# A mixer's opening: c's first convolution on other engines, first products in other banks, x's first turns behind the next x product

## What is computed

```python
proj = input_states @ in_proj_w.T              # 512 -> gate | x | B | C | dt
gate, xBC, dt = proj[..., :INTER], proj[..., INTER:INTER + CONV], proj[..., INTER + CONV:]
xBC = silu(causal_conv(xBC, conv_w, K=4) + conv_b)     # each channel by itself, 4 taps
hs, Bm, Cm = split(xBC)                        # x: 128 heads x 64;  B, C: 8 groups x 128
dt = softplus(dt + dt_bias);  cum = cumsum(dt * A)
scores = (C_i . B_j) * exp(cum_i - cum_j) * dt_j       # causal, for each head
y = scores @ x + D * x
g = rms_norm_by_group(y * silu(gate)) * norm_w
out = g @ out_w.T
```

## Time and profile before

| | us |
|---|---|
| median of 3 runs | 1915.48 (1914.93 to 1915.66) |
| profiled execution, its own time | 1914.4 |
| its span | 1912.7 |
| TensorE busy in the span | 1817.4 |
| GpSimd busy | 1434.0 |
| vector engine busy | 1340.3 |
| ScalarE busy | 1163.2 |

### The profile page before, as it was taken

The page is one execution under the profiler, slowest core; times in us unless marked ns, Lnnn a source line. Parts: engine busy times, 40 slices in busy tenths (PEclk is TensorE's granted clock), DMA queues, the critical chain, the costliest instruction groups (busy, mean ns, idle before and its releaser), DMA issues.

```text
span 1912.7 us, 29241 instructions
## 1 busy us (share of the span) xinstructions
PE 1817.4 (95%) x10780; PEld 1454.2 (76%) x10780; DVE 1340.3 (70%) x1703; ACT 1163.2 (61%) x2105; POOL 1434.0 (75%) x1429
## 2 busy tenths in 40 slices
PE   6998897878999999999999999999999999999977
PEld 4776675667887888888888888888888888888866
DVE  5664564666767777687668767876777687678656
ACT  3222432358676777676676757766777577676752
POOL 4312333638997999799969978997899799979972
PEclk9997997989999999999999999999999999999999
DMA  3000001013222222222222222222322223213201
GB/s 111 1 2 23 2 1 59 12 55 104 90 83 83 78 94 100 67 90 88 89 78 78 94 72 86 94 91 70 96 78 94 72 89 99 95 62 115 72 23 44
DMA packets 107025, 135.54 MB, mean 71 GB/s; under 512 B 9026, under 2 KB 74690, under 8 KB 106884
## 3 DMA queue, kind: packets, MB, share of 16 engines
q1 hardware_dynamic: 105924, 133.63, 21.3%
q10 hardware_dynamic: 960, 0.05, 0.0%
HBM read 131.02 MB, written 2.62 MB: 70 GB/s over the span
## 4 chain that ended last, share of the span: by engine, by line
PE 78%; DVE 2%; POOL 1%; issue 1%; ACT 1%; DVEq 0%; POOLq 0%; ACTq 0%
PE ps L144 20%; PE ps L146 20%; PE ps L145 20%; PE ps L1928 7%; PE ps L1885 3%; PE ps L1929 3%; PE ps L1074 2%; PE ps L1913 1%; PE ps L1946 1%; PE ps L1948 0%; DVE mix_xT L1667 0%; DVE mix_u L1791 0%; PE ps L116 0%; POOL ffn_ln_mv L72 0%; DVE mix_xnT_lo L132 0%
## 5 line engine op out<-in xcount | busy, mean ns | idle before, releaser
L144 PE MATMUL ps<-mix_xnT_hi,mix_w_hi 128*128 128x512 f32 x1152 | 463.1, 402 | 9.5 <-DVE mix_bT L1667 9.5
L146 PE MATMUL ps<-mix_xnT_hi,mix_w_lo 128*128 128x512 f32 x1152 | 455.5, 395 | 0.0
L145 PE MATMUL ps<-mix_xnT_lo,mix_w_hi 128*128 128x512 f32 x1152 | 455.1, 395 | 0.0
L1667 DVE SCALAR_TENSOR_TENSOR mix_xT<-ps,mix_cur,mix_xT 128x510 f32<-128x510 f32 x378 | 279.2, 745 | 144.1 <-ACT mix_xT L1482 135.1
L1393 POOL TENSOR_SCALAR_AFFINE_SELECT mix_spread<-mix_spread 128x256 f32<-128x256 f32 x512 | 305.7, 631 | 0.0
L1687 DVE TENSOR_TENSOR mix_decay<-mix_decay,mix_cb 128x1536 f32<-128x1536 f32 x128 | 293.8, 2333 | 4.9 <-ACT mix_decay L1508 4.7
L1531 ACT ACTIVATE mix_g_hi<-mix_gated 128x512 fp32r<-128x512 f32 x128 | 81.0, 633 | 328.3 <-POOL mix_gated L1370 173.2
L144 PEld LDWEIGHTS ps<-mix_xnT_hi,mix_w_hi 128*128 128x128 f32 x1152 | 217.8, 189 | 58.4 <-issue 11.1
L146 PEld LDWEIGHTS ps<-mix_xnT_hi,mix_w_lo 128*128 128x128 f32 x1152 | 217.4, 189 | 50.9
L145 PEld LDWEIGHTS ps<-mix_xnT_lo,mix_w_hi 128*128 128x128 f32 x1152 | 217.9, 189 | 47.1
L1506 ACT ACTIVATE mix_decay<-mix_spread,mix_cur_ncum 128x256 f32<-128x256 f32 x512 | 253.7, 495 | 0.0
(11 more groups left out here) (262 smaller groups left out, 3327.0 us busy)
## 6 DMA issues: line engine op xcount, KB each, us to landing
mix_spread<-cum_rows SPq DMA_DIRECT2D x128, 512.0 KB, 4.0
mix_w_raw<-in_w_in_stream SPq DMA_DIRECT2D x144, 256.0 KB, 4.2
mix_wo_raw<-in_w_out_T SPq DMA_DIRECT2D x64, 256.0 KB, 3.6
att_w_raw<-in_w_attn_T SPq DMA_DIRECT2D x12, 256.0 KB, 4.1
x<-in_x SPq DMA_DIRECT2D x8, 256.0 KB, 4.4
out_rows<-x SPq DMA_DIRECT2D x8, 256.0 KB, 2.1
att_wp_raw<-in_w_proj_T SPq DMA_DIRECT2D x4, 256.0 KB, 2.6
mix_bT<-in_w_ffn_T SPq DMA_DIRECT2D x2, 512.0 KB, 4.9
```

Of the source, the lines that this page charges most:

```text
L144: pe.matmul(out, lh, rh, start=(k == 0), stop=False)
L145: pe.matmul(out, lh, rl, start=False, stop=False)
L146: last = pe.matmul(out, ll, rh, start=False, stop=(k == tiles - 1))
L1667: dve.scalar_tensor_tensor(out=d[:, :, shift:T], in0=src[:, :, 0:T - shift], scalar=w[:, MK - 1 - shift:MK - shift], in1=d[:, :, shift:T], ...
```

## The change

Six things change, all in the opening (group 0, up to pair 0's x and B·C):

1. dt's turns go into banks 0, 1, 0, 1 instead of 6, 7, 4, 5; each waits for what that bank held (B's taps, or the copy of the turn before it).
2. Products 3 and 4 are issued by a new function `lead_product`, into banks 6, 7 and 4, 5, ahead of dt's turns.
3. C's taps 1 to 3 leave the vector engine: ScalarE scales each tap from the bank into one of four spare SBUF halves (`scale_c`), GpSimd adds it to `cT` (`add_c`). The semaphores are renumbered, so that `convolved` and `tapped` no longer count C.
4. x's turns (`turn_x`) move from ahead of the body to behind product 5.
5. In pair 0 of group 0 ScalarE takes x1's first tap ahead of the exponentials; the vector engine scales x (`scale_x`) and copies B·C 0 and 1 between x1's two halves of taps.
6. GpSimd's order: splits 3 and 4, two additions, split 5, four additions, split 6, then the body.

```diff
-        DT_BANKS = (6, 7, 4, 5)
+        DT_BANKS = (0, 1, 0, 1)
+        c_tapped, c_scaled, c_added = sem("c_tapped"), sem("c_scaled"), sem("c_added")
+        C_TAPS = [(half, shift) for half in range(2) for shift in range(1, MK)]
+        tapped_c = [ap[:, n * 512:(n + 1) * 512] for ap in (gated[:, 1, :], square[:, :]) for n in range(2)]
...
+            def add_c(n):
+                half, shift = C_TAPS[n]
+                pool.wait_ge(c_tapped, half + 1)
+                pool.wait_ge(c_scaled, n + 1)
+                at_least(pool, c_added, n)
+                by_batch = lambda ap: ap.rearrange("p (b t) -> p b t", t=T)
+                d = by_batch(cT[:, half * 512:(half + 1) * 512])[:, :, shift:T]
+                pool.tensor_tensor(d, d, by_batch(tapped_c[n % len(tapped_c)])[:, :, 0:T - shift], ALU.add)\
+                    .then_inc(c_added, 1)
...
             add_linear(1)
-            for n in range(4, LEAD + 2):
-                split_w(n, n, raw_uses(n))
+            split_w(4, 4, raw_uses(4))
+            add_c(0)
+            add_c(1)
+            split_w(5, 5, raw_uses(5))
+            for n in range(2, len(C_TAPS)):
+                add_c(n)
+            split_w(6, 6, raw_uses(6))
...
+            def scale_c(n):
+                half, shift = C_TAPS[n]
+                at_least(act, c_added, n + 1 - len(tapped_c))
+                act.activation(tapped_c[n % len(tapped_c)], ps[:, 2 + half, :], ACT.Identity,
+                               scale=lead_w[:, 2 * MK - 1 - shift:2 * MK - shift]).then_inc(c_scaled, 1)
...
+                    if first and k == 0:
+                        tap(0)
                     exps(g, k, 0, (0, 1))
-                    if has_next:
-
-                        if not (first and k == 0):
-                            act.wait_ge(y_gated, 2 * (PAIRS * g + k))
+                    if has_next and not (first and k == 0):
+                        act.wait_ge(y_gated, 2 * (PAIRS * g + k))
                         tap(0)
...
-            for n, dst in ((1, bT), (2, cT), (3, xT[:, 0, :])):
+            for n, dst, bank, done in ((1, bT, 0, tapped), (2, cT, 2, c_tapped)):
                 for half in range(2):
-                    tap0(n, dst, lead_w[:, (n - 1) * MK + MK - 1:(n - 1) * MK + MK],
-                         lead_w[:, 3 * MK + n - 1:3 * MK + n], half, 2 if n == 2 else 0)
+                    lead_tap(n, dst, half, bank, done)
+            scale_c(0)
+            lead_tap(3, xT[:, 0, :], 0, 6)
+            scale_c(1)
+            scale_c(2)
+            lead_tap(3, xT[:, 0, :], 1, 6)
+            for n in range(3, len(C_TAPS)):
+                scale_c(n)
             for n in range(4):
                 dt_to_rows(n)
-            for n, dst in ((1, bT[:, :]), (2, cT[:, :]), (3, xT[:, 0, :])):
-                silu_conv(n - 1, dst)
-            silu_gate(4, gated[:, 0, :])
+            silu_conv(0, bT[:, :])
+            act.wait_ge(c_added, len(C_TAPS))
+            act.activation(cT[:, :], cT[:, :], ACT.Silu).then_inc(silu_x, 1)
+            silu_conv(1, xT[:, 0, :])
+            silu_gate(4, gated[:, 0, :], 4)
...
-                    if k == 0:
+                    if k == 0 and not first:
                         take_cb(g, (0, 1))
                     if has_next:
                         conv_taps(n_conv(g, ("x", k + 1)), xT[:, (k + 1) % 2, :], cur_w(("x", k + 1)), 0)
+                    if k == 0 and first:
+                        scale_x(0, 0)
+                        take_cb(g, (0, 1))
...
-            for n, dst in ((1, bT), (2, cT), (3, xT[:, 0, :])):
-                for half in range(2):
-                    conv_taps(n - 1, dst, lead_w[:, (n - 1) * MK:n * MK], half, 2 if n == 2 else 0)
+            for half in range(2):
+                conv_taps(0, bT, lead_w[:, 0:MK], half, 0)
+            for half in range(2):
+                conv_taps(1, xT[:, 0, :], lead_w[:, 2 * MK:3 * MK], half, 6)
             dve.wait_ge(dt_out, 4)
-            scale_x(0, 0)
...
+            def lead_product(n, bank):
+                pe.wait_ge(w_lo_done, n)
+                for half in range(2):
+                    cols = slice(half * 512, (half + 1) * 512)
+                    three_pass(pe, ps[:, bank + half, :], lambda k: (w_hi[:, n % 2, k, :], w_lo[:, n % 2, k, :]),
+                               lambda k: (xnT_hi[:, k, cols], xnT_lo[:, k, cols])).then_inc(projected, 1)
...
+                if first and k == 0:
+                    pe.wait_ge(silu_g, 2)
                 pe.wait_ge(mixed, GHEADS * g + 2 * k + 2)
...
                         next_product(g, ("x", k + 1))
+                    if k == 0 and first:
+                        turn_x(0, 1, 0)
...
                 half, which = n // 2, n % 2
+                if n < 2:
+                    pe.wait_ge(convolved, 3 * n + 3)
+                else:
+                    pe.wait_ge(dt_out, n - 1)
                 pe.wait_ge(dt_step, CUM_READY * half + (DT_READY, CUM_READY)[which])
...
-            product(2, 2, ("conv", 1), (1,))
-            product(3, 3, ("conv", 2))
+            product(2, 2, ("c", 0), (1,))
+            lead_product(3, 6)
+            pe.wait_ge(dt_abs, 4)
+            lead_product(4, 4)
             for n in range(4):
                 turn_dt(n)
-            product(4, 4, ("gate", 0))
             pe.wait_ge(dt_out, 4)
-            turn_x(0, 2, 0)
             over_groups(body)
```

More of the change, by code:

```diff
@@ L1204, in n_conv @@
         def n_conv(g, item):
-            return LEAD - 2 + len(CONVS) * g + CONVS.index(item)
+            return 2 + len(CONVS) * g + CONVS.index(item)
         def n_gate(g, k):
@@ L1477, in _, with tap0 @@
         def _(act):
-            def tap0(n_prod, dst, w, bias, half, bank=0):
+            def tap0(n_prod, dst, w, bias, half, bank=0, done=tapped):
                 late = isinstance(n_prod, int) and (n_prod, half) == LATE
@@ L1482, in tap0 @@
                 act.activation(dst[:, half * 512:(half + 1) * 512], ps[:, bank + half, :], ACT.Identity,
-                               scale=w, bias=bias).then_inc(tapped, 1)
+                               scale=w, bias=bias).then_inc(done, 1)
             def silu_conv(n_cv, dst):
@@ L1487, in silu_conv, with silu_gate @@
                 act.activation(dst, dst, ACT.Silu).then_inc(silu_x, 1)
-            def silu_gate(n_prod, dst):
+            def silu_gate(n_prod, dst, bank=2):
                 for half in range(2):
                     act.wait_ge(projected, 2 * (n_prod - 1) + half + 1)
-                    act.activation(dst[:, half * 512:(half + 1) * 512], ps[:, 2 + half, :], ACT.Silu).then_inc(silu_g, 1)
+                    act.activation(dst[:, half * 512:(half + 1) * 512], ps[:, bank + half, :], ACT.Silu)\
+                       .then_inc(silu_g, 1)
+            def scale_c(n):
[3 more added lines that the diff above has]
+                               scale=lead_w[:, 2 * MK - 1 - shift:2 * MK - shift]).then_inc(c_scaled, 1)
             def cur_conv(item):
@@ L1637, in _, with lead_tap @@
             dt_factors(1)
-            for n, dst in ((1, bT), (2, cT), (3, xT[:, 0, :])):
+            def lead_tap(n, dst, half, bank, done=tapped):
+                tap0(n, dst, lead_w[:, (n - 1) * MK + MK - 1:(n - 1) * MK + MK],
+                     lead_w[:, 3 * MK + n - 1:3 * MK + n], half, bank, done)
+            for n, dst, bank, done in ((1, bT, 0, tapped), (2, cT, 2, c_tapped)):
                 for half in range(2):
-                    tap0(n, dst, lead_w[:, (n - 1) * MK + MK - 1:(n - 1) * MK + MK],
-                         lead_w[:, 3 * MK + n - 1:3 * MK + n], half, 2 if n == 2 else 0)
+                    lead_tap(n, dst, half, bank, done)
[6 more added lines that the diff above has]
+                scale_c(n)
             for n in range(4):
                 dt_to_rows(n)
-            for n, dst in ((1, bT[:, :]), (2, cT[:, :]), (3, xT[:, 0, :])):
-                silu_conv(n - 1, dst)
-            silu_gate(4, gated[:, 0, :])
+            silu_conv(0, bT[:, :])
[3 more added lines that the diff above has]
+            silu_gate(4, gated[:, 0, :], 4)
             over_groups(body)
@@ L1868, in product @@
                         pe.wait_ge(silu_g, 2 * count + half + 1)
+                    if kind == "c":
+                        pe.wait_ge(c_scaled, 3 * half + 3)
                     cols = slice(half * 512, (half + 1) * 512)
@@ L1878, in turn_x @@
             def turn_x(uses, conv, buf):
-                pe.wait_ge(silu_x, conv + 1)
+                pe.wait_ge(silu_x, conv + 2)
                 for half in range(2):
@@ L1939, in b_dot_c @@
             def b_dot_c(g, batches):
-                pe.wait_ge(silu_x, n_conv(g, CONVS[0]))
+                pe.wait_ge(silu_x, n_conv(g, CONVS[0]) + 1)
                 for b in batches:
@@ L2026, in _ @@
             mln.turn_pe(pe, 6)
-            product(2, 2, ("conv", 1), (0,))
+            product(2, 2, ("c", 0), (0,))
             mln.turn_pe(pe, 7)
```

## The result

The changed kernel takes **1906.52 us** (median of 8 runs, 1900.1 to 1908.26) against 1915.16 for the kernel before in the same rounds (8 runs, 1908.59 to 1916.23): ratio 0.9953, 95% interval 0.9942 to 0.9964. The forecast was 1906.0, its range 1903.0 to 1910.5.

What follows compares the result with a forecast made beforehand. TensorE, busy 1817.4 of 1912.7 us, was taken as the bound, with its waits in the mixer's opening. Saving 8.9 + 0.6 = 9.5 us from 1914.4 gave 1904.9, or 1906.0 on the median's scale; range 1903.0 to 1910.5.

Steps and rivals of the forecast that it cites:

- The banks: Opening: product 3 starts at 398.05 without waiting for b's taps; the 9.5 us hole and 2.6 us of half clock go.
- (b): Rival: no contention on the vector engine and a warm clock; saving 10.6 us, 1904.9 us, chance 0.17.
- dt's turns: Opening: the four turns follow product 4 in banks 0 and 1; undisturbed, x1's product starts at 412.4 instead of 423.85.
- Contention: Vector engine: GpSimd's first additions slow dt's two scans by 0 to 1.7 us, taken as 1.0; y 8.9 us early.
- Additions: GpSimd: c's additions take 1.7 us for the first two and 1.35 for the rest, done at 414.0, before silu of c.
- The new wait ahead of B·C: TensorE, behind x's turns: a new wait of 2.3 us, 418.85 to 421.2, for x scaled by dt.
- (c): Rival: GpSimd's additions become the bound, the gain gone at 3.1 us per addition; slower or equal, chance 0.03.
- (a): Rival: the clock falls in a new TensorE hole; before the first gate half it adds 2.6 us; 1908.6 us, chance 0.22.
- From x1 to y: Opening, undisturbed: x1's product starts at 412.4, decay products take 3.9 us, and y starts at 431.0 after a 2.0 us wait.
- (d): Rival: x's turns and b·c wait a whole further step, some 5 us; saving 4 to 5 us, 1911 us, chance 0.10.
- Pair 1: Behind pair 0's y: a further 0.5 to 0.7 us gained if the clock holds, and no later wait takes it back.
- The total: Whole kernel: saving 9.5 us, 8.9 at pair 0's y and 0.6 in pair 1, giving 1906.0 us; chance 0.45.

Runs made afterwards that it cites:

- e4: The changed kernel with x's turns and their scaling put back ahead of x1's product: 1915.87 us against 1914.56 before, ratio 1.0007.
- e2: The changed kernel with one more wait, so GpSimd starts c's additions only when dt's last scan is done: 1904.36 us, ratio 0.996 to before.
- e5: The changed kernel with never-read matmuls among dt's turns, behind x's turns and ahead of pair 0's y: 1907.55 us, ratio 0.9964 to before.
- f1: The changed kernel run a third time, no edit: 1906.62 us against 1913.78 before, ratio 0.9964.
- f2: The same program as e2 run again, c's additions waiting for dt's scans: 1905.31 us against 1913.78 before, ratio 0.9957.
- e3: The kernel before with c's convolution alone moved to ScalarE and GpSimd, TensorE's order and banks as before: 1921.33 us, ratio 1.0038 to before.
- e0_after: The changed kernel run again for a second trace, no edit: 1907.55 us against 1911.73 before, ratio 0.9973.
- e1_banks_only: The changed kernel with c's taps back on the vector engine, everything else as changed: 1907.2 us against 1911.73 before, ratio 0.9984.

## Why the prediction was right or wrong, step by step

- **The banks (right).** Product 3 starts at 389.76, that is 398.00 on before's scale, forecast 398.05. The hole and its half clock are gone. That this gives time only because x's turns move behind x1 is shown by e4. In the prediction (b)'s saving of 10.6 should be 10.5 by its own terms; nothing hangs on it.
- **dt's turns (right, but for the contention).** Without it x1 stands at 412.42 (e2), forecast 412.4.
- **Contention (the mis-sized term).** Taken at 1.0 us with an upper bound of 1.7 for the scans; it is 2.5 (0.91 on the scaling, 1.60 on the scans), of which 1.9 to 2.0 reach pair 0's y at equal clock (e5 against e2, f1 against f2). Two steps failed. The scans were taken to suffer less because they ask for operands at half the pace; they slowed by a factor of 2.26, about as much as the upper end of L1791 (2.3). Each scan took either 0.66 to 0.69 us or 1.46 to 1.49, so there was no price between. And the sum left out the scaling between L1791's steps and the scans, which has one SBUF input, and which slowed most of all, 2.9 times. The rule that I cited in the Trainium skill (GPSIMD Engine Reference, Specifications) names a two-port mode beside two SBUF inputs, and the Trainium skill (VectorE: DVE Perf Modes, "Mode 2×_2P — use both read ports for one tensor") puts one-source operations of the tensor_scalar kind between SBUF tensors into that mode. The traces agree: 0.49 alone and 1.40 beside an addition; the taps, which read a bank, stay at 4.5 for six. I quoted the whole rule, applied the half that fitted the scans, and did not go through the vector engine's queue with the other half.
- **Additions (right).** 1.74 for the first, forecast 1.7; 1.09 for the second, also forecast as 1.7; 1.08 to 1.27 for the rest, forecast 1.35. Silu of c stands without a wait, as forecast. Rival (c) had nothing to stand on in this order; e3 shows that GpSimd's queue can bring c late by its order, not by the price of an addition.
- **The new wait ahead of B·C (right, with the clock deciding where it shows).** 2.29 in e0_after and f1_after, forecast 2.3. In the profiled execution of after it is 0.44, because x1's product itself ran at the lower level and filled it.
- **Rival (a) (it happens).** The low clock behind that wait stands in e0_after and f1_after, with y 1.59 and 0.64 us later than in after, and 2.20 and 1.25 later than in the warm e5_filled, of a forecast 2.6. Some 0.9 of e0's stand already at x1's start (26.48 us behind the anchor, 25.57 in f1), behind turns of dt at the low clock. The case before x1 was forecast as hidden but for 0.4, and after's trace has it: B·C starts 9.25 us behind x1, where the forecast has 8.8 and the two traces with a warm x1 have 9.02 and 9.01. I gave (a) 0.22; its costly form stands in two of three traces, the hidden one in the third.
- **From x1 to y.** Forecast 18.6 us, measured 19.28: 0.45 from the clock, 0.35 more for the four B·C blocks and their copies, 0.27 less for the decay products (3.63 instead of 3.9), and 0.15 in gaps around them. The hole ahead of y was forecast as 2.0 and is 1.57. The row names ScalarE, whose gate silu had ended at 425.40; the decay products ended at 426.24 and released it.
- **Rivals (b) and (d).** (b) needs a vector engine without contention, which only e2's added wait gives. (d) did not come about: x is scaled between x1's halves of taps (415.49 in after's trace). Its price, 4.5 to 5.5 us of the saving, is of the size of what e4 lost with the turns in the wrong place (4.7 to 6.7), but that is another order than (d)'s.
- **Pair 1 (right in direction).** 1.03 us were gained where 0.6 were forecast: 7.37 at pair 1's y against 6.34 at pair 0's (1.4 in e0_after and in f1_after). In f1_after the clock fell there and pair 1's gain turned into a small loss (5.44 of 5.70 us left at x's turns). The middle of the mixer kept the rest: 1383.54 and 1383.48 us. That the two agree so closely is partly chance: in the other runs it took 1381.17 to 1385.24.
- **The total (luck had a part).** Pair 0's y was forecast 8.9 us early and is 6.34 early in after. The 2.6 between are 1.5 more contention than priced, 0.4 of low clock among dt's turns (x1 at 415.31 instead of 414.9) and 0.7 from x1 to y. The sum said 9.5 us; the openings say 7.4, 6.2 and 5.4. That the first median fell on 1906.5 was partly luck, and owes something to the stages outside: over the three rounds of measurement the changed kernel is 6.7 us under before on the mean, which is about what the openings give (6.3). On the scale of 1915.5 that would be 1909, in the range but 3 us from the forecast.

What stays open: what makes the stages outside the opening move from one execution to another, and why the low clock falls where it does. The traces show only that low clock stands where the time is lost: e0_after, at the anchor 7.7 us later than after, has 0.81 granted in 320:380 where after has 0.92, and before has 0.91 in 200:320 where after has 0.98.

## What to carry to other kernels

Before work is given to GpSimd, go through the vector engine's queue beside its new place and price every instruction there that has only SBUF operands, one input or two, by the end of the GpSimd instruction that it starts beside (here that end and another 0.3 to 0.55 us), not by its own length; a step that waits for the end of that stretch can cost little and give most of it back (here 2.5 us on the vector engine and 1.9 to 2.0 at pair 0's y, though the kernels' times don't yet tell the two apart). A bank or an engine that is freed early pays only if independent work stands behind the next dependency: move that work first (here x1's product ahead of x's turns was worth 4.7 to 6.7 us of the opening, some 2 of them the low clock behind the hole). And compare a stage from an anchor inside the kernel, in more than one execution, before a total is read as proof of a sum.

## What the runs showed of the hardware

- A vector operation with **one** SBUF input was slowed more beside GpSimd (0.49 to 1.40 us) than one with two (scans, 1.27 to 2.87 for two). A single scan took either 0.66 to 0.69 us or, beside GpSimd, 1.46 to 1.49, and nothing between, in all traces. The slowed ones ended 0.54 to 0.55 us behind the end of a GpSimd instruction, the slowed scaling 0.28 to 0.30; GpSimd's own addition took 1.74 instead of 1.29. Operations with an input in a bank kept their pace (0.75 each).
- Holes of 2.1 to 2.9 us on TensorE lost the clock in some executions of a program and kept it in others. Behind the same 2.85 us ahead of B·C the clock stayed up in e2_adds_wait and fell in f2_wait. Pair 1's y behind a hole of 2.14 us was warm in e0_after and behind 2.13 at the 1.2 GHz level in f1_after (4.46 us to x's turns; 2.77 in e1_banks_only, warm behind the same 2.13). Behind 2.52 it was warm in after.
- The stretch up to the anchor, the same code in all kernels, took from 380.66 to 389.31 us, the middle of the mixer from 1381.17 to 1385.24, and the stretch behind the last y from 66.82 to 69.46.
